# Layer 2 of a two-layer recurrent network: the transposes of the keys moved ahead of the spread norms, and VectorE's products of the keys ahead of those of the queries

## The reference

```
q = l2_normalize(xn @ Wq);  k = l2_normalize(xn @ Wk);  v = xn @ Wv
alpha = sigmoid(xn @ Wg + bg)
la_cum = cumsum(log(alpha)) within a chunk;  la_mean = la_cum.mean(-1)
decay = exp(la_mean[:, None] - la_mean[None, :]) * tril
o_intra = (q k^T * decay) v
kv_chunk = (k * exp(la_cum[last] - la_cum))^T v
o_inter = (q * exp(la_cum)) S,   S = S * exp(sum log alpha) + kv_chunk
x = x + (o_intra + o_inter) @ Wo;  x = x + gelu(LN(x) @ W1 + b1) @ W2 + b2
```

## Time and profile before

| | |
|---|---|
| median of 3 runs (lowest to highest) | 2049.53 us (2042.01 to 2052.2) |
| the profiled execution | 2047.19 us, its span 2045.2 us |
| mean granted clock of PE | 0.961 |
| busy: PE matmul, PE weight load | 1741.8 us (85%), 1255.9 us (61%) |
| busy: DVE, ACT, POOL | 1280.8 us (63%), 996.9 us (49%), 220.7 us (11%) |

### The profile page before, as it was taken

The page is one execution under the profiler, slowest core; times in us unless marked ns, Lnnn a source line. Parts: engine busy times, 40 slices in busy tenths (PEclk is TensorE's granted clock), DMA queues, the critical chain, the costliest instruction groups (busy, mean ns, idle before and its releaser), DMA issues.

```text
span 2045.2 us, 60865 instructions
## 1 busy us (share of the span) xinstructions
PE 1741.8 (85%) x23060; PEld 1255.9 (61%) x23060; DVE 1280.8 (63%) x3518; ACT 996.9 (49%) x2242; POOL 220.7 (11%) x235
## 2 busy tenths in 40 slices
PE   5999999998999999958888888886889899889562
PEld 3665666556666666735666666765666676666562
DVE  5677777775766666656666766766666666665311
ACT  2444444444555555534655456553555454555242
POOL 0000000000000000020111011101111110110122
PEclk9899999998999999989999999998999999999887
DMA  4222222222222112221221222110122211111473
GB/s 141 86 95 95 95 95 95 95 95 81 62 74 73 44 53 74 96 95 45 73 68 56 68 70 77 55 37 24 62 64 65 65 60 46 49 56 39 159 245 112
DMA packets 97579, 160.62 MB, mean 79 GB/s; under 512 B 14729, under 2 KB 66057, under 8 KB 94090
## 3 DMA queue, kind: packets, MB, share of 16 engines
q1 hardware_dynamic: 88170, 135.05, 20.1%
q0 software_dynamic: 9248, 23.17, 3.7%
HBM read 96.45 MB, written 61.69 MB: 77 GB/s over the span
## 4 chain that ended last, share of the span: by engine, by line
PE 53%; DVE 16%; issue 11%; ACT 9%; SPq 5%; DMA 3%; POOL 2%; DVEq 0%; ACTq 0%; POOLq 0%
PE psum L920 5%; PE psum L799 4%; PE psum L777 3%; PE psum L1224 3%; PE psum L910 3%; PE psum L1115 3%; PE psum L1074 2%; PE psum L808 2%; PE psum L959 2%; PE psum L844 2%; PE psum L1012 2%; PE psum L848 2%; PE psum L1140 2%; PE psum L1005 2%; PE psum L1044 2%
## 5 line engine op out<-in xcount | busy, mean ns | idle before, releaser
L1455 ACT ACTIVATE pts<-psum 128x512 f32<-128x512 f32 x192 | 99.1, 603 | 170.6 <-PE psum L959 170.0
L684 POOL DMA_INDIRECT rows<-h,recA x64 | 64.3, 1004 | 828.8 <-DVE recA L1680 699.6
L1942 DVE TENSOR_REDUCE mneg<-psum 128x2 f32<-128x512 f32 (+1 forms) x192 | 119.1, 684 | 54.7 <-PE psum L939 35.2
L920 PE MATMUL psum<-wa,xT_s 128*128 128x512 f32 x256 | 122.7, 625 | 0.0
L799 PE MATMUL psum<-txT,wt 128*128 128x128 f32 x864 | 116.7, 278 | 5.7 <-DVE st L1949 3.0
L708 POOL DMA_INDIRECT rows<-xn,recC x32 | 34.7, 1083 | 751.2 <-DVE recC L2122 647.3
L1074 PE MATMUL psum<-xT_s,wa 128*128 128x256 f32 x512 | 115.7, 380 | 0.0
L799 PEld LDWEIGHTS psum<-txT,wt 128*128 128x128 f32 x864 | 107.9, 195 | 8.9 <-DVE st L1949 4.0
L1074 PEld LDWEIGHTS psum<-xT_s,wa 128*128 128x128 f32 x512 | 96.3, 191 | 13.0 <-issue 0.8
L808 PE MATMUL psum<-wt,tg 128*128 128x128 f32 x528 | 78.4, 279 | 16.5 <-DVE tg L1647 16.5
L1645 DVE TENSOR_TENSOR tg<-tg,psum 128x256 f32<-128x256 f32 x84 | 35.2, 419 | 78.0 <-ACT tg L1319 77.1
(11 more groups left out here) (276 smaller groups left out, 4292.1 us busy)
## 6 DMA issues: line engine op xcount, KB each, us to landing
wt<-in_wB SPq DMA_DIRECT2D x84, 384.0 KB, 2.9
outs<-pbd SPq DMA_DIRECT2D x16, 1024.0 KB, 7.0
wt<-in_wD SPq DMA_DIRECT2D x24, 578.0 KB, 3.5
wa<-in_wD SPq DMA_DIRECT2D x15, 578.0 KB, 3.6
tx<-rows SPq DMA_DIRECT2D x132, 64.0 KB, 2.9
outs<-ty SPq DMA_DIRECT2D x132, 64.0 KB, 1.6
rows<-pbd SPq DMA_DIRECT2D x64, 128.0 KB, 1.8
rows<-pbd SPq DMA_DIRECT2D x8, 1024.0 KB, 3.9
```

The source lines that it names most:

```text
L920: mm(bank(f"{name}{t}{c}"), xnT[:, t * P:(t + 1) * P], wqkv0[:, off + c * 512:off + (c + 1) * 512], start=True, stop=True).then_inc(*fills ...
L1455: af(pT[:, n, :], bank(f"e{n}"), ACT.Exp, scale=float(HD) ** -0.5).then_inc(*frees(f"e{n}"))
L1942: ins = v.tensor_reduce(mneg[:, int(n >= 4), col:col + hs], sc, AX.X, ALU.max, negate=True)
```

## The change

The diff, whole, with the code around it shortened:

```
         names += [f"tv{t}{c}" for t in range(NT) for c in range(2)]
-        names += ["rkT"] + [f"rb{j}" for j in range(4)]
+        names += ["rkT"]
+        names += [f"tk{t}{c}" for t in range(NT) for c in range(2)]
+        names += [f"rb{j}" for j in range(4)]
         names += [f"la{j}" for j in range(4)]
-        names += [f"tk{t}{c}" for t in range(NT) for c in range(2)]
         tile_step(2)
...
                 last.then_inc(*fills("rkT"))
+                for t in range(NT):
+                    for c in range(2):
+                        pe.wait_ge(*emptied(f"tk{t}{c}"))
+                        for a in range(4):
+                            last = tr(bank(f"tk{t}{c}")[:, a * P:(a + 1) * P], kT[:, 4 * c + a, t * P:(t + 1) * P])
+                        last.then_inc(*fills(f"tk{t}{c}"))
                 for j in range(4):
                     pe.wait_ge(*emptied(f"rb{j}"))
...
-                for t in range(NT):
-                    for c in range(2):
-                        pe.wait_ge(*emptied(f"tk{t}{c}"))
-                        for a in range(4):
-                            last = tr(bank(f"tk{t}{c}")[:, a * P:(a + 1) * P], kT[:, 4 * c + a, t * P:(t + 1) * P])
-                        last.then_inc(*fills(f"tk{t}{c}"))
                 tile_step(2)
...
-                for j in range(4):
-                    dve.wait_ge(*filled(f"rb{j}"))
-                    s = slice(2 * j, 2 * j + 2)
-                    v.scalar_tensor_tensor(out=qt[:, s, :], in0=bank(f"rb{j}").rearrange("p (a n) -> p a n", a=2), scalar=1e3, in1=qt[:, s, :], op0=ALU.mult, op1=ALU.mult).then_inc(*frees(f"rb{j}"))
                 for t in range(NT):
                     for c in range(2):
                         dve.wait_ge(*filled(f"tk{t}{c}"))
                         dve.wait_ge(*read_out(f"te{t}{c}"))
                         s = slice(c * 512, (c + 1) * 512)
                         v.tensor_tensor(kd[:, t, s], kd[:, t, s], bank(f"tk{t}{c}"), ALU.mult).then_inc(*frees(f"tk{t}{c}"))
+                for j in range(4):
+                    dve.wait_ge(*filled(f"rb{j}"))
+                    s = slice(2 * j, 2 * j + 2)
+                    v.scalar_tensor_tensor(out=qt[:, s, :], in0=bank(f"rb{j}").rearrange("p (a n) -> p a n", a=2), scalar=1e3, in1=qt[:, s, :], op0=ALU.mult, op1=ALU.mult).then_inc(*frees(f"rb{j}"))
                 tile_step(2)
```

## The result

The changed kernel takes 2057.57 us (median of 9 runs, 2051.59 to 2068.59) against 2049.53 us (2042.01 to 2053.47, 9 runs) before: ratio 1.0044, 95% interval 1.0023 to 1.0066. That is 8.0 us more; the forecast was 6.0 us more, at 2055.5. Its profiled execution took 2056.60 us with a span of 2054.9 us. PE is busy for 1752.7 us, VectorE for 1279.1 us, ScalarE for 995.6 us, all as before within 1%.

A forecast was written before the change was run, and what follows sets the result against it. PE and VectorE were taken to keep the same pace from norms to scores, with the PSUM banks deciding the waits. 3.0 + 3.6 - 0.6 = 6.0 us gave 2053.2, as a median 2055.5 us; range 2045 to 2067.

The forecast's parts named there:

- The banks, and where the wait goes: Spread norms: the new bank order moves PE's wait to the last product of the values, some 1.35 us again.
- The D round: Rounds with three tiles of the second mixture: th1 and scores 0.37 us later, 8 rounds, 3.0 us.
- The B round: Rounds with six tiles of the first mixture: ScalarE's gate 0.52 us later, 7 rounds, 3.6 us.
- The round without tiles: Keys' transposes run in PE's slow-clock stretch, so the scores start earlier: -0.6 us, bounds -0.6 to +0.4.
- The instruction supply, taken at zero: PE's gaps no engine causes: between 5.9 us vanishing and 18 us added in the decays, taken as zero.
- My rival for this: Decays, tight against the scores, find the instruction buffer empty in most rounds: +18 us, 2073, or half, 2065; chance 0.15.
- such holes would be swallowed there: Behind the scores: the DVE wait ahead of the outputs swallows holes there, but not those in the decays.
- the pace: The three round terms together, D, B and without tiles: 3.0 + 3.6 - 0.6 = 6.0 us.
- The page of the Trainium skill: PE's instruction fetch in blocks of 256, mostly hidden behind issue: by that rule the order costs nothing, sum 6.0 us.

The follow-up runs named there:

- e1: The changed kernel with VectorE's old order (queries' products before the keys'), PE's order and banks as changed: 2134.3 us in one run.
- e2: The changed kernel with the last product of the values cut from 64 to 1 column a head: 2052.60 us, ratio 1.0002 to the kernel before.
- e3: The kernel before with the last product of the values cut from 64 to 1 column a head: 2054.48 us, ratio 1.0005.
- the shifted pair: The kernel before and the changed one, each with 128 semaphore instructions added ahead of PE's first layer-2 round: 2062.49 and 2072.58 us.
- e8: The changed kernel measured once more, with a second profile: 2057.64 us, ratio 1.0018 to the kernel before at 2052.89 us.
- the pairs with the early norms: Old and changed order, norms transposed after two of four products of the values: 2031.34 and 2045.88 us; with 128 added semaphore instructions 2064.95 and 2077.27 us.
- the last pair: Old and changed order, both with norms transposed after two products of the values and 128 added semaphore instructions: 2064.95 and 2077.27 us.
- e4: The kernel before with the norms transposed after two of the four products of the values: 2031.34 us, ratio 0.9895.
- e9: The kernel before with 128 semaphore instructions added once ahead of PE's first round of layer 2: 2062.49 us, ratio 1.0043.

## Why the prediction was right, and where it was not

- **The banks, and where the wait goes.** Right. The spread norms wait for the last product of the values, 1.29 us (1.35 said), behind the keys' transposes, and the small waits stand inside the decays. e1 showed the tie through the decays' banks, e2 and e3 that VectorE paces the changed order and PE the old one.
- **The D round.** 0.37 us said, 0.32 to 0.33 measured. The release of the spread norms took 0.22 us here instead of the 0.26 I had used for each. 8 rounds make 2.6 us in place of 3.0.
- **The B round.** 0.52 us said, 0.33 measured at the scores and 0.35 at VectorE's gate (1285.05 is 9.04 us behind VectorE's copy of the norms, and it was 8.70 before). The mechanism shows: ScalarE takes the tile straight behind the decays, and VectorE's gap grows (to 1.45 us, 1.6 said). The term was too large, since the second half of the decays ended 0.1 us sooner than in my walk and ScalarE queued less. 7 rounds make 2.3 us in place of 3.6.
- **The round without tiles.** -0.6 us said; from the norms' transpose to the scores it went from 9.60 to 8.76 us, -0.8. Its rows in the changed kernel:

```profile
1411.80 4.10 PE L778 MATMUL psum<-ident,reg 128*128 128x128 f32 x18 [7.53 <-ACT reg L1496]
1415.83 1.60 PE L1134 MATMUL psum<-reg,headrow 32*128 32x256 f32 x16
1417.36 2.10 PE L1147 MATMUL psum<-tri,big 64*64 64x64 f32 x128
```

  The transposes fill the slow stretch, the wait is gone, and the decays already take the 2.10 us that they take elsewhere. The pause ahead, for ScalarE's inverse norms, is 7.53 us in place of 8.64; the prediction did not have this, and in the shifted pair it goes the other way (7.4 and 8.3 us).
- **The instruction supply, taken at zero.** This is the term that was mis-sized. With the terms above alone the loss would be 2.6 + 2.3 - 0.8 = 4.1 us, and e8's 4.8 would fit, but the first comparison had 8.0, the shifted pair 10.1, and the pairs with the early norms 12 to 15 us. The gaps rise by 7 to 9 us between the kernel before and the changed one, and by 17 us in the last pair. Part of that was free here: PE's waits for VectorE's states behind the scores (L1200 and L1213 before, 6.3 and 5.8 us) shrank to 2.8 and 2.1 us, which fits holes that fell into them. My rival for this had put the holes into the decays, where they stayed at 4 and became shorter (5.9 to 4.0 us); they came behind the scores. I had argued that such holes would be swallowed there, and they are only in part.
- **The total.** That 6.0 lay near 8.0 came of two errors of opposite sign: the pace was taken 1.9 us too high (6.0 against 4.1) and the supply some 4 us too low. That it came so near was luck. By the traces, in which the rounds lose 6.7 us, the supply is worth some 3 to 4 us, and the intervals of the two comparisons (1 to 7 and 5 to 14 us) leave room for both.
- **The page of the Trainium skill** ("Runtime: NRT & Kernel Launch", section Instruction fetch mechanics) says that fetching in blocks of 256 instructions is mostly hidden. The runs bear out the blocks (one transfer of 16384 bytes for some 256 instructions), but not that they are hidden in this stream: 15 to 37 us in gaps over the rounds, nine tenths of them ending just behind such a transfer, and moving all code by half such a block moved the holes to other rounds.

What stays open: why the changed order has more holes. Decays and scores (256 instructions each in 2.1 us) now stand closer together and the 16 slow transposes no longer lie between them: from the start of the decays to the start of the scores of an undisturbed D round PE issues 330 matmuls and weight loads in 6.16 us before and 298 in 4.74 us after, 54 and 63 a microsecond. That fits transfers that never start less than 3.27 us apart, but no run changed the spacing alone.

## What to carry to other kernels

When banks are given out in the order of a list, a step moved ahead takes free banks from the one behind it. Write down for each use whose bank it gets before you count a filled gap as a gain; here the wait moved to a later product of the same row. Ask which engine paces a stretch by cutting half a microsecond of one engine's work in both versions (e2, e3), and then start that engine's row earlier (e4: -1.05%) instead of reordering what waits for it. In long written-out streams of small matmuls the order also decides how long PE waits for its own instructions, so compare two versions at more than one place of the code, and hold the gaps named "issue" against the transfers of instructions.

## What the runs showed of the hardware that I had not expected

- 128 semaphore instructions, written out once in PE's stream, follow each other by 0.15 us (from 931.45 to 951.09 us in e9). Part of this passes under matmuls that still run, and PE's gap grew from 4.0 to 15.9 us.
- A pause of 3.77 us of PE was followed by 5 us at a granted clock of 0.50, and 128 small matmuls took 3.70 us instead of 2.1; in the 16 rounds of e1 they took 3.3 to 4.4 us. A pause of 1.3 us did this in no round of the changed kernel by itself, and in one with a hole of 1.54 us behind it.
- PE's instructions come in transfers of 16384 bytes, never started less than 3.27 us apart in the rounds, and 346 of 386 gaps "issue" of 0.3 us or more end 1.1 to 1.65 us after the end of one.
- One change shifts the whole later code, and with it which rounds have holes: D rounds of the kernel before differ by up to 1.9 us from the values to the scores, and in both profiles of the changed kernel the same rounds have the holes in this stretch.
